# A two-layer graph kernel: E of the next tile ahead of G on ScalarE, row sums by accumulator output, squares on ScalarE, and new tables of places

## The reference

```
# layer 0: attention inside blocks of 64 nodes, then a three-layer MLP
Wh = x @ W;  e = leaky(Wh @ a, 0.2)
scores = softmax(diagonal 64x64 blocks of adj * e)
o = scores @ Wh;  z = MLP(o) + o;  z = layernorm(z) * g + b
x1 = layernorm(x + z)
# layer 1: 4 heads, dense attention over 2048 x 2048
h = x1 @ W_proj.T
s = leaky(s_left[i] + s_right[j] + adj[i, j] * we, 0.2), masked where adj <= 1e-5
agg = softmax(s over j) @ h
out = layernorm(x1 + leaky(x1 + agg + bias, 0.5))
```

## Time and profile before

| | |
|---|---|
| median of 3 runs | 1992.19 us (1987.78 to 1993.39) |
| the profiled execution | 1992.15 us, its span 1990.3 us |
| busy in the span | PE 1804.3, DVE 1865.5, ACT 1547.9, POOL 1863.7 us |
| first tile on POOL starts, last one ends | 76.1, 1970.6 us |
| busy of these 1894.5 us | PE 1741.8, DVE 1829.7, ACT 1494.3, POOL 1841.0 us |
| a body, start to start on POOL | 242.2, 239.2, 238.4, 239.4, 239.2, 238.4, 234.8, 222.9 us |
| mean granted TensorE clock | 0.981 |

### The profile page before, as it was taken

How to read it: one execution, slowest core, us unless ns; L and a number is a source line. 1 busy time by engine, 2 the same in 40 slices (tenths; PEclk the granted TensorE clock), 3 DMA queues, 4 the chain that set the end, 5 groups by cost and what they waited for, 6 DMA issues and landing times.

```text
span 1990.3 us, 34086 instructions
## 1 busy us (share of the span) xinstructions
PE 1804.3 (91%) x11080; PEld 883.8 (44%) x11080; DVE 1865.5 (94%) x3557; ACT 1547.9 (78%) x3415; POOL 1863.7 (94%) x663
## 2 busy tenths in 40 slices
PE   7799998999989998999989998999998999888885
PEld 6544444444444444445444444444444444333332
DVE  3699999999999998999989999899999999999997
ACT  6678887898778887788878888788887897666664
POOL 3599999999999999999999999999999999999996
PEclk8899999999999999999999999999999999999999
DMA  3233324233243243333233332333324233233310
GB/s 100 73 112 94 101 70 134 85 119 100 68 118 112 85 120 99 93 101 109 80 99 119 86 110 87 99 115 95 101 70 129 90 112 91 89 109 91 109 51 11
DMA packets 138088, 190.61 MB, mean 96 GB/s; under 512 B 22328, under 2 KB 56504, under 8 KB 137912
## 3 DMA queue, kind: packets, MB, share of 16 engines
q1 hardware_dynamic: 137912, 188.44, 32.0%
HBM read 179.77 MB, written 8.65 MB: 95 GB/s over the span
## 4 chain that ended last, share of the span: by engine, by line
DVE 43%; PE 23%; issue 18%; POOL 12%; ACT 2%; SPq 0%; DVEq 0%; DMA 0%; ACTq 0%; POOLq 0%
DVE X L1110 30%; PE psum L1229 19%; POOL X L499 11%; DVE X L1099 5%; PE psum L1408 4%; DVE st L936 1%; DVE x1s L993 1%; POOL haug L482 1%; DVE res L1053 1%; DVE est L936 1%; DVE psum L1044 1%; DVE lky L1059 1%; ACT o_sb L662 1%; DVE mv L942 1%; ACT E L765 0%
## 5 line engine op out<-in xcount | busy, mean ns | idle before, releaser
L499 POOL TENSOR_TENSOR X<-RHO,E 128x1536 f32<-128x1536 f32 (+1 forms) x512 | 1776.4, 3504 | 55.9 <-ACT E L765 51.2
L1110 DVE SCALAR_TENSOR_TENSOR X<-psum,s_j,X 128x512 f32<-128x512 f32 x2048 | 1397.7, 738 | 49.4 <-POOL X L499 44.7
L1229 PE MATMUL psum<-X,haug 128*33 128x512 f32 x4096 | 991.3, 605 | 3.1 <-DVE X L1110 3.1
L765 ACT ACTIVATE E<-psum,we_s 128x512 f32<-128x512 f32 x512 | 396.9, 775 | 264.4 <-PE psum L1229 263.1
L1408 PEld LDWEIGHTS psum<-ident,adj_sb 128*128 128x128 f32 x2048 | 287.8, 141 | 589.7 <-DVE X L1110 442.4
L1408 PE MATMUL psum<-ident,adj_sb 128*128 128x128 f32 x2048 | 434.1, 293 | 123.5 <-DVE X L1110 120.9
L1229 PEld LDWEIGHTS psum<-X,haug 128*33 128x33 f32 x4096 | 196.4, 111 | 429.9 <-issue 393.7
L768 ACT ACTIVATE psum<-psum,we_s 128x512 f32<-128x512 f32 x512 | 380.9, 744 | 0.0
L1229 PE MATMUL psum<-sgn_ident,pen 128*128 128x128 bf16 x2048 | 377.5, 221 | 0.0
L726 ACT ACTIVATE pen<-adj_sb,pen_bias 128x512 bf16<-128x512 f32 x512 | 367.2, 717 | 0.4
L1099 DVE TENSOR_TENSOR X<-psum,E 128x512 f32<-128x512 f32 x496 | 333.5, 672 | 4.7 <-ACT psum L561 2.3
(11 more groups left out here) (227 smaller groups left out, 1446.7 us busy)
## 6 DMA issues: line engine op xcount, KB each, us to landing
adj_sb<-in_adj_dram SPq DMA_DIRECT2D x128, 1024.0 KB, 5.2
RHO<-rho_scratch SPq DMA_DIRECT2D x31, 1024.0 KB, 9.8
out_dram<-o_sb SPq DMA_DIRECT2D x32, 256.0 KB, 2.9
xg<-in_x_dram SPq DMA_DIRECT2D x28, 256.0 KB, 5.6
blk<-in_adj_dram SPq DMA_DIRECT2D x56, 64.0 KB, 5.3
X<-in_x_dram SPq DMA_DIRECT2D x2, 256.0 KB, 3.0
W_sb<-in_L_gnn_W_dram SPq DMA_DIRECT2D x4, 64.0 KB, 1.9
X<-in_adj_dram SPq DMA_DIRECT2D x4, 64.0 KB, 2.8
```

Of the source, the lines that this page charges most:

```text
L499: Q.tensor_tensor(X[m % NX][:, 0:heads, :], RHO[:, g % 2, 0:heads, :], bc(E[m % NE][:], 1, [P, heads, GROUP]), ALU.mult).then_inc(B_pool, 1)
L765: A.activation(E[m % NE][:], TA[m % NT], ACT.Exp, scale=we_s[:, 3:4], bias=we_s[:, 5:6]).then_inc(E_sb, 1)
L1110: ins = V.scalar_tensor_tensor(slot[:, h, :], TA[m % NT], s[:, k, h:h + 1], slot[:, h, :], ALU.mult, ALU.max)
L1229: return T.matmul(o, l, r, start=start, stop=stop)
```

## The change

Four things are done at once.

- **Order of E and G.** In ACT's loop the entry of tile m makes E of m and then G of m - 1, where G of m stood. What stood between the two (`copy_RB` at k = 1, `epi_acc` at k = 2) now stands ahead of G of m - 1. One G is made behind the loop.
- **Sums.** `bn_stats` and `bn_aggr` go, save for the four chains of the first batch. The residual's four `scalar_tensor_tensor` on DVE write a row sum through an accumulator output. `lky`, which was one `tensor_tensor` of 128 x 512, becomes four `scalar_tensor_tensor` of 128 x 128 with row sums.
- **Squares.** ACT's `invstd` now makes -sum/128, four Square activations of 128 x 128 from SBUF with that as bias and an accumulator output, then Ln and Exp.
- **Tables.** Most tables and `FOUR` have new entries.

```diff
-    FOUR = (7, 35)
+    FOUR = (11, 29)
...
-    AT_PE = {"xT": (-26, -19, 0, 18), ... "y1": (-9, 11, 22, 33), "y2": (-8, 12, 23, 34), ...
+    AT_PE = {"xT": (-26, -20, 0, 18), ... "y1": (-9, 11, 22, 33), "y2": (-8, 12, 24, 34), ...
-    AT_ACT = {... "wh1": (-21, -13, 8, 21), ... "y1": (-6, 14, 25, 36), "y2": (-5, 15, 26, 36), ...
+    AT_ACT = {... "wh1": (-21, -13, 9, 22), ... "y1": (-6, 14, 25, 35), "y2": (-5, 14, 27, 36), ...
-    AT_DVE = {"max": (-20, -9, 10, 25), "rin": (-16, -8, 13, 27), "res": (0, 19, 30, 41), "r_stats": (2, 20, 33, 42)}
+    AT_DVE = {"max": (-20, -13, 12, 26), "rin": (-18, -6, 16, 27), "res": (1, 19, 30, 42)}
-    ONCE_SP = {"rho": 54}
-    EPI_PE = {"back0": 1, "back1": 3}
+    ONCE_SP = {"rho": 49}
+    EPI_PE = {"back0": 2, "back1": 3}
-    EPI_DVE = {"part0": 3, "part1": 5, "stats": 7}
-    EPI_POOL = {"shift": 12}
+    EPI_DVE = {"part0": 4, "part1": 5, "lky": 6}
+    EPI_POOL = {"shift": 15}
...
-            def invstd(log, out, minus, mean_var):
-
-                A.activation(log, mean_var[:, :, 1], ACT.Ln, bias=eps_c[:])
-                link(copy(minus, mean_var[:, :, 0], -1.0))
+            def invstd(log, out, minus, sums, sq, src):
+
+
+                link(copy(minus, sums, -1.0 / D))
+                for t in range(GT):
+                    ins = A.activation(squares[:, t, :], src(t), ACT.Square, bias=minus[:, t:t + 1],
+                                       accum_out=sq[:, t:t + 1])
+                link(ins)
+                link(A.activation(log, sq, ACT.Ln, scale=1.0 / D, bias=eps_c[:]))
                 return A.activation(out, log, ACT.Exp, scale=-0.5)
...
-                if m >= NT:
-                    make_G(m)
+                if m > NT:
+                    make_G(m - 1)
...
+                if c >= NB + 2:
+                    dve.wait_ge(rstd_r, prev(c) - NB + 1)
                 for t in range(GT):
                     ins = V.scalar_tensor_tensor(x1_of(c)[:, t, :], mid_bank(c)[:, tsl(t)], rstd[s][:, t:t + 1],
-                                                 xb[s][:, t, :], ALU.mult, ALU.add)
+                                                 xb[s][:, t, :], ALU.mult, ALU.add,
+                                                 accum_out=rsum[s][:, t:t + 1])
...
-                V.tensor_tensor(lky[:], BK_B.rearrange("p (t f) -> p t f", t=GT), x1_of(g)[:], ALU.add).then_inc(lky_sb, 1)
+                for t in range(GT):
+                    ins = V.scalar_tensor_tensor(lky[:, t, :], BK_B[:, tsl(t)], 1.0, x1_of(g)[:, t, :], ALU.mult, ALU.add,
+                                                 accum_out=esum[:, t:t + 1])
+                ins.then_inc(lky_sb, 1)
```

More of the change, by code:

```diff
@@ L135, in build_program @@
         lky = sb("lky", [P, GT, D])
[L136 to L137 removed]
+        esum = sb("esum", [P, GT])
+        esq = sb("esq", [P, GT])
+        squares = sb("squares", [P, GT, D])
         elog = sb("elog", [P, GT])
@@ L187, in build_program @@
         ssq = [sb(f"ssq{v}", [P, GT]) for v in range(6)]
-        st6 = [sb(f"st6{v}", [P, GT, 6]) for v in range(6)]
-        mv = [sb(f"mv{v}", [P, GT, 2]) for v in range(6)]
+        first_st = [sb(f"first_st{c}", [P, GT, 6]) for c in U]
+        first_mv = [sb(f"first_mv{c}", [P, GT, 2]) for c in U]
+        rsum = [sb(f"rsum{v}", [P, GT]) for v in range(6)]
+        rsq = [sb(f"rsq{v}", [P, GT]) for v in range(6)]
         lg = [sb(f"lg{v}", [P, GT]) for v in range(6)]
@@ L932, in _ @@
             V = nc.vector
-            def moments(st, src, done):
-                for t in range(GT):
-                    ins = V.bn_stats(st[:, t, :], src(t))
-                ins.then_inc(done, 1)
-            def mean_var(st, out, ready, count, done):
-                dve.wait_ge(ready, count)
-                for t in range(GT):
-                    V.bn_aggr(out[:, t, :], st[:, t, :]).then_inc(done, 1)
             def first_logits(c):
@@ L961, in first_zn, with first_moments, first_var @@
                 ins.then_inc(zn_first, 1)
+            def first_moments(c):
+                wait_r(dve, c)
+                for t in range(GT):
+                    ins = V.bn_stats(first_st[c][:, t, :], x1_of(c)[:, t, :])
+                ins.then_inc(st_first, 1)
+            def first_var(c):
+                dve.wait_ge(st_first, c + 1)
+                for t in range(GT):
+                    V.bn_aggr(first_mv[c][:, t, :], first_st[c][:, t, :]).then_inc(var_first, 1)
             def first_norm(c):
                 s = set_of(c)
-                dve.wait_ge(rstd_r, c + 1)
+                dve.wait_ge(rstd_first, c + 1)
                 for t in range(GT):
-                    ins = V.tensor_scalar(x1_of(c)[:, t, :], x1_of(c)[:, t, :], mv[s][:, t, 0:1], rstd[s][:, t:t + 1],
+                    ins = V.tensor_scalar(x1_of(c)[:, t, :], x1_of(c)[:, t, :], first_mv[c][:, t, 0:1], rstd[s][:, t:t + 1],
                                           ALU.subtract, ALU.mult)
@@ L1079, in epilogue @@
                         (epi_rden, epi_scale, epi_add)[part](g - 1, r)
-                if k == EPI_DVE["stats"]:
-                    (epi_lky, epi_moments, epi_var)[part](g - 1)
+                if k == EPI_DVE["lky"] and part == 0:
+                    epi_lky(g - 1)
             def tile(m):
@@ L1132, in host @@
                             residual(c)
-                        if n == AT_DVE["r_stats"][u] and part < 2:
-                            (r_moments, r_var)[part](c)
                     if n == ONCE_DVE["rm"] and part == 0:
```

82 lines of the change are left out of this document (31 added, 51 removed), and 6 rows, old and new, of the table AT_PE.

## The result

The changed kernel takes 1998.95 us, the median of 7 runs, against 1991.41 of before (1987.25 to 1993.39, 7 runs on the same chip). The ratio is 1.0038, with a 95% interval of 1.0028 to 1.0048: slower by 0.4%, where the forecast was 1978 and faster. Six of the seven runs lie between 1997.49 and 2000.00 us; one read 3510.93 and is left out of the ratio.

What follows compares the result with a forecast made beforehand. POOL and DVE were taken to bound the loop together, PE close behind. From 1992.15 us, -13.7 - 7.7 + 2 + 7 + 0.6 and -2.5 gave 1978 us; range 1952 to 2008, the forecast's own 1968 to 1986 (chance 0.40).

Steps and rivals of the forecast that it cites:

- the order of E and G: ACT's queue: late G costs DVE 33 us at group boundaries, about the 37 DVE wins; no gain or loss counted.
- Mostly it is hidden under DVE's tile m - 1: Away from group boundaries, DVE needs G 4.0 us after X_sb and gets it 2.4 after at best.
- this stall goes, -13.7 us: Tile 57: lky made ahead of tile 54 ends PE's 2.91 us wait and POOL's stall, -13.7 us over six bodies.
- the -7.7: Tile 37: y1 of chain 3 moved to tile 35 cuts POOL's wait from 1.38 to 0.3 us, in seven bodies.
- the 21 us for the reads: DVE: 236 accumulator outputs at 0.09 us each add 21 us of work; bounds nothing and 0.15 us each.
- the relief: DVE: less work away from the boundaries leaves E more allowance in small waits, 0.35 us a body, -2.5 us.
- +7 for ACT's bursts: ACT: norms on heavy tiles that follow each other, 1 us at one place in each of seven bodies; bounds 0 and 50.
- the norms and the end: ACT's bursts +7, DVE's lighter load -2.5, and the last norm of all, slower by moving to ACT, +0.6 us.
- That the gains cancel: Rival: waits at 57 and 37 only move, behind bursts at tiles 22 to 28 and 49 to 51; 1992 us, chance 0.19.
- The slow rival: ACT's queue: overrun of 0.9 us paid at each of eight norms a body; 2021 us, 1996 at half; chance 0.23.
- The first rival: DVE's relief counts in full, POOL alone bounds, its idle falls to about 3 us a body; 1960 us, chance 0.18.
- The +2 at tile 14: Chain 1 has y1 and y2 on one ACT tile, the old fault of tile 37: 0.3 us a body, +2 us.

Runs made afterwards that it cites:

- experiment 6: The kernel before with only lky and its norm one tile earlier (k = 6 for 7): 1994.40 us, ratio 1.0017.
- experiment 5: The kernel before with the new tables alone, bn_stats kept and old order: 2005.47 us, ratio 1.0070.
- experiments 9 and 10: Changed kernel in the old order, one norm back on DVE: the output's (1988.59 us, ratio 0.9990), then that of x1 (1990.14 us, 0.9995).
- experiment 1: The changed kernel with the old order, G of tile m made in ACT's entry m again: 1982.48 us, ratio 0.9956.
- experiment 12: The kernel of experiment 1 with FOUR, the tiles where POOL makes all four heads, at (37, 49) for (11, 29): 1971.39 us, ratio 0.9903.
- 11: The kernel of experiment 1 with ACT's x1T of chain 0, r_norm of chain 3 and h1 of chain 2 moved one tile: 1980.76 us, ratio 0.9947.

## Why the prediction was wrong

**Two steps failed, a third was off the other way, and the first sets the sign.** That is the one on the order of E and G: "DVE gives back at the group boundaries (33) about what it wins (37) ... and I give this part alone no gain." The lateness of G was seen and sized, and then cancelled against DVE's relief, so that the order stood at nothing in the sum. It doesn't cancel. The order costs 16.5 us in the changed kernel and 13 to 29 in the other three pairs. Without it the kernel is at 1982.5 us, 4.5 above the forecast and faster than before.

**Its size was right at the boundaries and left out the rest.** 33 us were counted, at the boundaries only, 4.3 in body 3. There they have 4.6 us of waits, 1.04 for the 2.3 taken at tile 17 and 2.58 for the 1.5 at tile 49. But DVE waits 63.1 us for G over the run, 8.8 in body 3, so about half stands at other tiles, and a third of the loss (5.7 of 16.5 us) lies elsewhere. "Mostly it is hidden under DVE's tile m - 1" left out what the old order had in its favour: G of m stood ahead of ACT's host work of that tile, and now stands behind it, as the rows at tile 49 show.

**The second failed step is in the tables:** "this stall goes, -13.7 us", and likewise the -7.7. The stall at tile 57 went, as it said. The one at 37 only spread out: 1.19 of its 1.38 us stand at tiles 35 to 37 with the tables alone, where a wait of 0.3 was reckoned at tile 37 and none beside it. The time didn't go: experiment 6 has the one move alone at +3 us, and experiment 5 the tables alone at +14, where the sum had -19.4. POOL's idle time was read as a set of separate stalls with separate causes. The runs fit one budget better: body 3 has 7.6 us of it before, 7.5 in the changed kernel, 7.8 in experiment 5 and 7.3 in 6, wherever the stalls stand. DVE has 230.7 us of work in a body against POOL's 231.8 and regains 0.2 us in a plain tile; that it gets the rest of its catching up only while POOL stands is argued from this, not shown by a run of its own. A single figure for the tables doesn't exist: beside the norms they gain 2.2%.

**The norms were valued wrongly.** ACT got 99 us where 106 were taken; the burst measures 2.38 us for 2.4. DVE lost 46 us in the page, for 37. The groups of DVE in the loop:

```profile
L1061 DVE SCALAR_TENSOR_TENSOR lky<-psum,x1s 128x128 f32<-128x128 f32 x124 | 28.7, 287 | 8.3 <-ACT psum L758 8.0
...
L1061 DVE DVE_READ_ACCUMULATOR lky<-psum,x1s 128x1 f32 x124 | 10.3, 83 | 0.0
L1005 DVE DVE_READ_ACCUMULATOR x1s<-psum,rstd,xb 128x1 f32 x112 | 9.1, 81 | 0.0
```

`lky` is 28.7 / 124 = 0.23 us apiece, for the 0.280 taken from the earlier trace rows. The accumulator reads have rows of their own; that an op with an accumulator output is two instructions is also what the Trainium skill says (VectorE: DVE Perf Modes, Two Vector instructions with no wait between them). The trace agrees, with 236 rows of 0.08 us. But the rows must not be added up: the next instruction starts where the read starts. The residual's four, before and in the changed kernel:

```profile
866.83 1.12 DVE L993 SCALAR_TENSOR_TENSOR x1s<-psum,rstd,xb 128x128 f32<-128x128 f32 x4
867.87 0.68 DVE L1099 TENSOR_TENSOR X<-psum,E 128x512 f32<-128x512 f32 x1
```

```profile
869.20 0.34 DVE L1005 SCALAR_TENSOR_TENSOR x1s<-psum,rstd,xb 128x128 f32<-128x128 f32 x1
869.46 0.08 DVE L1005 DVE_READ_ACCUMULATOR x1s<-psum,rstd,xb 128x1 f32 x1
869.46 0.34 DVE L1005 SCALAR_TENSOR_TENSOR x1s<-psum,rstd,xb 128x128 f32<-128x128 f32 x1
...
870.27 0.68 DVE L1092 TENSOR_TENSOR X<-psum,E 128x512 f32<-128x512 f32 x1
```

Four take 867.87 - 866.83 = 1.04 us without reads and 870.27 - 869.20 = 1.07 with them, about 0.01 us a read where 0.09 was taken. So the 21 us for the reads were mis-sized; the reads are near the prediction's lower bound, nothing. (The reads behind `lky` can't be compared so, since its instructions changed shape.) On the other side the norms' groups also count overlapping ends: from start to start four `bn_stats` take 0.78 us (826.15 to 826.93 in the trace of before) and four `bn_aggr` 0.29 (827.58 to 827.87), so 59 norms were some 63 us of DVE's work and not 72.3. What remains between these prices and the 46 us wasn't taken apart.

I counted the relief as worth 2.5 us, and +7 for ACT's bursts. With the new tables the norms are worth 1.14% = 23 us, so the relief is worth 23 us more than the bursts cost.

**The account of the changed kernel**, then, along one path: tables +14, norms -23, order +16.5, in all +7.5. The forecast had -19.4 for the tables, +5.1 for the norms and the end, and nothing for the order. The tables are 33 us worse than forecast and the order 16.5, the norms 28 better. That 1999 lies in the stated range is therefore luck: large errors partly cancel. Another path shares the same total out otherwise (norms +34, tables -43, order +16.5), so the shares hold for their path only. Two slips in the prediction's arithmetic change nothing: 862.28 - 860.05 is 2.2, and 0.66 + 0.61 + 0.66 is 1.93.

**The rivals.** None is borne out whole. That the gains cancel named the places: in body 3 POOL waits 1.16 us at tile 23, 0.38 at 28 and 1.28 at 50 and 51. But it put them down to the bursts. With the tables alone, without the new squares, the waits at 28, 50 and 51 are the same (0.37, 1.07, 0.22), and in the old order that at 23 is 0.33:

```profile
873.52 3.46 POOL L501 TENSOR_TENSOR X<-RHO,E 128x1536 f32<-128x1536 f32 x1 [0.33 <-ACT E L773]
```

So the tables and the order make nearly all of these waits. The slow rival has the right sign, and at half its price the nearest number, 1996. Its ground was ACT's bursts, and experiments 9 and 10 show that handing a norm from ACT back to DVE makes the kernel slower. Its mechanism isn't nothing, though: the 0.83 us at tile 38 stand behind a burst, and with the old tables the norms cost 34 us. The Trainium skill's rule (ScalarE: Activation LUTs, Rules for kernel authors: add and mul to VectorE) argues from the speed per element. The price of one instruction agrees: a square 0.39 us, a `bn_stats` 0.22. As a rule on placement it isn't borne out here: the engine with 45 us to spare in a body is ACT. The first rival, DVE's relief in full, asked for POOL's idle time to fall by 31.5 us. Without the order it falls by 11.7 (experiment 1), and with `FOUR` moved too by 22.3 (experiment 12), so the order alone didn't hold it back.

**The signs.** DVE down by 37 (46) and ACT up by 106 (99) held; so did no PE wait for `lky`. "New waits of DVE's products on ACT's G, up to 2 us at k = 1" held in kind, at 2.6 us. "POOL's idle in the loop from 53.5 to about 40" failed, at 57.9. POOL's waits grew at tiles 23 and 50, one of the named ways to be wrong. An accumulator output didn't cost over 0.15 us, and DVE does wait for G. The +2 at tile 14 didn't come: POOL waits 0.04 us at tile 15.

What stays open is why the norms cost as much as 34 us with the old tables. The pile-up at tile 35, with the clock's fall in two bodies, makes POOL's waits at tile 37 12.7 us longer over the run. Further waits appear (0.67 and 0.76 us at tiles 23 and 24, 1.23 at 27, 1.02 at 59 in body 3), which I didn't take apart. Open, too, is why the tables alone lose most of their time in the last two bodies.

## What to carry to other kernels

Where two engines of a ring are nearly equally full, the idle time of the one can be the catching-up time of the other. In experiments 5, 6 and 11 a stall that was taken away came back at other tiles; less work on the late engine, or useful work put into the stall, did shorten the loop. Look for a removed wait at the tiles beside it before it is called gone. Before a lateness is set off against a relief, ask whether both act at the same instruction, and when a producer is moved behind other work on its queue, count all that stands ahead of it there, not only the neighbour that the edit names. Parts of a change should be tried in all combinations when places were chosen for the whole: here the tables alone lost 0.7%, the norms alone 1.7%, and both together gained 0.4%. And the price of a small instruction is read from the starts of its neighbours, with it and without it, not from its row.
